# Quadratic attention inside a three-part kernel: the features are regrouped into four pairs of heads, and the second half's moments are taken earlier

## The reference, cut to what matters

```
q, k, v = split(x @ Wqkv.T + bqkv)            # 8 heads x 8 channels each
qn = normalize(q) * (scale * temperature); kn = normalize(k) * scale
v1 = [1, v]                                   # 9 columns a head
kv_mod[i,j,e] = sum_n kn_i kn_j v1_e / N      # moments of second degree
kv[d,e] = sum_n kn_d v1_e / N;  vsum[e] = sum_n v1_e / N
y = 0.5 * qn_i qn_j kv_mod[i,j,:] + scale^2 * qn_d kv[d,:] + scale^4 * vsum
out = (y[1:] / y[0]) @ Wproj.T + bproj
```

## Time and profile before

| | |
|---|---|
| median of 3 runs | 777.17 us (777.17 to 780.46) |
| profiled execution | 778.77 us |
| its span in the trace | 776.9 us |
| TensorE busy | 712.7 us, 92% |
| VectorE busy | 542.0 us, 70% |
| GpSimd busy | 439.9 us, 57% |
| ScalarE busy | 425.0 us, 55% |

### The profile page before, as it was taken

How to read it: one execution, slowest core, us unless ns; L and a number is a source line. 1 busy time by engine, 2 the same in 40 slices (tenths; PEclk the granted TensorE clock), 3 DMA queues, 4 the chain that set the end, 5 groups by cost and what they waited for, 6 DMA issues and landing times.

```text
span 776.9 us, 11085 instructions
## 1 busy us (share of the span) xinstructions
PE 712.7 (92%) x3474; PEld 354.0 (46%) x3474; DVE 542.0 (70%) x859; ACT 425.0 (55%) x763; POOL 439.9 (57%) x402
## 2 busy tenths in 40 slices
PE   5699999999999896869999999889999999999997
PEld 2345454544445453327777778523333333333332
DVE  2399899999899898775588888494444545454543
ACT  1788777878786885523455554544343333333342
POOL 1388777877787766845566666234443434343440
PEclk9799999999999997869999999999999999999999
DMA  4365465434444553331000000644944434443400
GB/s 132 128 165 148 128 155 143 123 95 114 111 123 124 132 131 82 80 87 24 2 1 4 3 5 3 128 94 93 183 99 108 99 75 92 107 105 77 89 1 21
DMA packets 30098, 70.20 MB, mean 90 GB/s; under 512 B 4483, under 2 KB 20175, under 8 KB 29647
## 3 DMA queue, kind: packets, MB, share of 16 engines
q1 hardware_dynamic: 29727, 68.77, 36.6%
q10 hardware_dynamic: 304, 0.63, 0.2%
HBM read 66.96 MB, written 2.43 MB: 89 GB/s over the span
## 4 chain that ended last, share of the span: by engine, by line
PE 46%; DVE 8%; issue 1%; ACT 1%; DVEq 0%; ACTq 0%
PE pair L849 22%; PE pair L930 11%; PE pair L790 5%; PE pair L773 3%; PE pair L826 2%; PE pair L813 1%; PE pair L835 1%; PE pair L841 1%; DVE big L1563 1%; DVE big L1567 1%; DVE big L1629 0%; DVE big L1628 0%; DVE big L1575 0%; DVE big L1568 0%; DVE big L1883 0%
## 5 line engine op out<-in xcount | busy, mean ns | idle before, releaser
L1726 DVE TENSOR_TENSOR hidden<-pair,tmp 128x502 f32<-128x502 f32 (+1 forms) x192 | 121.5, 674 | 127.4 <-PE pair L849 102.6
L1857 POOL TENSOR_TENSOR hidden<-xs,big 128x502 f32<-128x502 f32 (+1 forms) x96 | 111.9, 1167 | 163.4 <-PE pair L849 144.0
L1276 ACT ACTIVATE tmp<-pair 128x502 f32<-128x502 f32 (+1 forms) x192 | 102.4, 586 | 154.5 <-PE pair L849 154.5
L1883 POOL TENSOR_TENSOR big<-big 94x512 f32<-94x512 f32 (+3 forms) x120 | 89.2, 781 | 58.2 <-DVE big L1628 58.2
L849 PE MATMUL pair<-xs,w 64*128 64x502 f32 (+1 forms) x384 | 106.5, 631 | 0.0
L849 PE MATMUL pair<-hidden,w 64*128 64x502 f32 (+1 forms) x384 | 97.7, 585 | 4.3 <-DVE hidden L1726 3.3
L1418 DVE TENSOR_TENSOR_SCAN pair<-tmp,pair 128x750 f32<-128x750 f32 (+1 forms) x56 | 95.8, 1712 | 7.9 <-ACT tmp L1020 7.6
L930 PE MATMUL pair<-hidden,w 128*64 128x502 f32 (+1 forms) x384 | 91.1, 596 | 0.0
L1748 POOL TENSOR_TENSOR big<-big,work 128x750 f32<-128x750 f32 (+1 forms) x28 | 45.8, 1634 | 78.4 <-ACT big L994 78.4
L501 PE MATMUL pair<-big,work 128*128 128x512 f32 x112 | 62.2, 638 | 2.1 <-DVE work L1430 2.0
L849 PEld LDWEIGHTS pair<-hidden,w 64*128 64x128 f32 x384 | 36.6, 187 | 50.8 <-issue 46.1
(11 more groups left out here) (189 smaller groups left out, 1235.6 us busy)
## 6 DMA issues: line engine op xcount, KB each, us to landing
big<-dispatched SPq DMA_DIRECT2D x40, 502.0 KB, 6.6
spread<-rowsd SPq DMA_DIRECT2D x48, 375.0 KB, 5.6
spread<-rowsd SPq DMA_DIRECT2D x48, 187.5 KB, 3.3
big<-in_x SPq DMA_DIRECT2D x12, 375.0 KB, 6.3
big<-dispatched SPq DMA_DIRECT2D x8, 498.0 KB, 5.8
spread<-rowsd SPq DMA_DIRECT2D x8, 374.0 KB, 4.9
w<-in_w SPq DMA_DIRECT2D x5, 512.0 KB, 6.7
big<-in_x SPq DMA_DIRECT2D x1, 1500.0 KB, 8.1
```

What stands on the lines that cost most here:

```text
L1276: act.activation(sT[i % 4][:, 0:w], bank[BANK1[i]][:, 0:w], ACT.Silu).then_inc(silu_a, 1)
L1726: v.tensor_tensor(hidT[i % 8][:, 0:hi - lo], bank[BANK2[i]][:, 0:hi - lo], sT[i % 4][:, 0:hi - lo], ALU.mult)\
L1857: pool.tensor_tensor(xw[e % 4][:, 0:hi - lo], xs[:, lo:hi], wx[:, e, 0:hi - lo], ALU.mult)\
L1883: ins = eng.tensor_tensor(dst[:, :, at:at + H * m].rearrange("p u (h d) -> p u h d", d=m), t[:, :, :, 0:m], t[:, :, :, k:D], ALU.mult)
```

## The change

The features are regrouped by head: 36 products, 8 linear, 1 one for each head (HF = 45). A tile now holds two heads (FT = 90) and there are four tiles (FTN = 4). q, k and v lie in `qkv` with nine columns a head, the ninth a one, so that [v, 1] of two heads is 18 neighbouring columns.

- `moments(n)` swaps the operands: stationary are 32 columns of v and ones around a pair's 18, moving the 90 features of k; 16 products, four of them in a row each writing another 32 partitions of bank 4. Rows and columns that belong to other heads are multiplied by zero: VectorE multiplies once by `featw` (128x180) into `kvT`.
- `moments_turned(n)` is new on TensorE: two products `kvT`^T x `ksel` turn this back, pick each head's columns and copy the denominator to 8 columns. ScalarE copies the result into `kvm` (`moments(n)` on ScalarE, new).
- `q_features(n)`: 16 transposes and four copies.
- `attend(n)`: 16 products with a stationary 90x32 and 188 moving columns, four in a row each for another pair of heads and another 32 partitions of the bank. A stationary holds one sequence's 16 columns beside 16 of zeros; the two sequences are accumulated.
- `moments(2*att+1)` moves on TensorE and VectorE ahead of `project`, `gates`, `residual`, `logits` and `qk_sums`. It waits for ScalarE's copy of the first half's moments, since both halves now use bank 4.
- `wproj` has its rows by pair of heads and sequence and comes in 8 small transfers in place of 2; `featw` is built on GpSimd instead of loaded.

```diff
-QUAD = 288
-FEATS = QUAD + 72
-FT, FTN = 120, 3
+QUAD = 36
+HF = QUAD + D + 1
+FEATS = H * HF
+FT, FTN = 2 * HF, H // 2
+VW = 2 * (D + 1)
+VAT = [144 + VW * g - 14 for g in range(FTN)]
...
+            return (bank[2], bank[3], attended(n), bank[4 if n % 2 else 5])[f]      # features_bank(n, f)
...
             def moments(n):                                   # TensorE
...
-                if n % 2:
-                    after(pe, att_v, n - 1)
-                else:
-                    after(pe, kv_v, n - 1)
+                after(pe, kv_a, n)
+                after(pe, qt_a, FTN * n if n % 2 == 0 else 0)
                 for b in range(2):
-                    for f in range(FTN):
-                        for p in range(2):
-                            at = 65 * (FTN * b + f)
-                            mm = pe.matmul(bank[4 + n % 2][0:FT, at:at + 65],
-                                           kF[r % 2][0:rows, unit, FT * f:FT * f + FT],
-                                           qkv[r % 2][0:rows, unit, 143:208], start=(p == 0), stop=(p == 1))
+                    for p in range(2):
+                        for g in range(FTN):
+                            mm = pe.matmul(bank[4][32 * g:32 * g + 32, FT * b:FT * b + FT],
+                                           qkv[r % 2][0:rows, unit, VAT[g]:VAT[g] + 32],
+                                           kF[r % 2][0:rows, unit, FT * g:FT * g + FT], start=(p == 0), stop=(p == 1))
+            def moments_turned(n):
+                pe.wait_ge(fw_g, 3)
+                pe.wait_ge(kt_v, n + 1)
+                for b in range(2):
+                    mm = pe.matmul(bank[4][0:FT, 256 + 128 * b:384 + 128 * b], kvT[:, FT * b:FT * b + FT], ksel[:, :],
+                                   start=True, stop=True)
+                mm.then_inc(kc_p, 1)
...
             def attend(n):                                    # TensorE
                 for k in range(2):
-                    for f in range(FTN):
-                        for b in range(2):
-                            mm = pe.matmul(dst[64 * b:64 * b + 64, TOK * k:TOK * k + TOK],
-                                           kvm[n % 2][:, k, FTN * b + f, :], qT[n % 2][:, f, TOK * b:TOK * b + TOK],
-                                           start=(f == 0), stop=(f == FTN - 1))
+                    for b in range(2):
+                        for g in range(FTN):
+                            mm = pe.matmul(dst[32 * g:32 * g + 32, TOK * k:TOK * k + TOK],
+                                           kvm[n % 2][:, g, k, b:b + 2, :].rearrange("p b c -> p (b c)"),
+                                           qT[n % 2][:, g, TOK * b:TOK * b + TOK], start=(b == 0), stop=(b == 1))
...
             def attention():                                  # TensorE, order of a round
...
+                    if att is not None:
+                        moments_turned(2 * att)
+                        moments(2 * att + 1)
                     if ln2 is not None:
                         project(ln2)
                     if gate is not None:
                         gates(gate)
                     if att is not None:
-                        moments(2 * att + 1)
+                        moments_turned(2 * att + 1)
...
+            def moments(n):                                   # ScalarE
+                act.wait_ge(kc_p, n + 1)
+                after(act, at_p, n - 1)
+                src = bank[4][0:FT, 256:512].rearrange("p (b q c) -> p q b c", b=2, c=16)
+                dst = kvm[n % 2].rearrange("p g k b c -> p (g k) b c")[:, :, 0:3:2, :]
+                act.activation(dst, src, ACT.Copy).then_inc(kv_a, 1)
...
+                    if att is not None:                       # ScalarE, order of a round
+                        moments(2 * att)
                     if qkvs is not None:
                         qk_squares(qkvs)
                     if gate is not None and gate + 1 < NQ:
                         gate_exponentials(gate)
                     if qkvs is not None:
                         qk_norms(qkvs)
+                    if att is not None:
+                        moments(2 * att + 1)
                     if ln2 is not None:
                         second_squares(ln2)
...
             def moments(n):                                   # VectorE
                 v.wait_ge(kv_p, n + 1)
-                after(v, at_p, n - 1)
-                src = bank[4 + n % 2][0:FT, 0:2 * FTN * 65].rearrange("p (f c) -> p f c", c=65)
-                v.tensor_tensor(kvm[n % 2][:, 0], src[:, :, 1:65], featw[:, :, :], ALU.mult)
-                v.tensor_tensor(kvm[n % 2][:, 1], src[:, :, 0:1].to_broadcast([FT, 2 * FTN, 64]), featw[:, :, :],
-                                ALU.mult).then_inc(kv_v, 1)
+                after(v, kc_p, n)
+                v.wait_ge(fw_g, 2)
+                v.tensor_tensor(kvT, bank[4][:, 0:2 * FT], featw[:, :], ALU.mult).then_inc(kt_v, 1)
...
+                    if att is not None:                       # VectorE, order of a round
+                        moments(2 * att + 1)
                     if ln2 is not None:
                         residual(ln2)
                     if gate is not None:
                         logits(gate)
                     if qkvs is not None:
                         qk_sums(qkvs)
-                    if att is not None:
-                        moments(2 * att + 1)
```

More of the change, by code:

```diff
@@ L201, in features_bank, with of_heads @@
         def features_bank(n, f):
-            return attended(n) if f == FTN - 1 else bank[2 + f]
+            return (bank[2], bank[3], attended(n), bank[4 if n % 2 else 5])[f]
+        def of_heads(t, at, count):
+            return t[:, :, at:at + (D + 1) * count].rearrange("p u (h d) -> p u h d", d=D + 1)[:, :, :, 0:D]
         def dispatchT(r):
@@ L266, in program @@
             blk = slice(64 * k, 64 * k + 64)
-            later += [(wqkv[blk, 192 * k:192 * k + 192], a["wqkv"]), (wproj[blk, blk], a["wproj"]),
+            later += [(wqkv[blk, 192 * k:192 * k + 192], a["wqkv"]),
                       (gatew[blk, NE * k:NE * k + NE], a["gate_w"])]
@@ L271, in program @@
             (centering, "centering"), (averaging, "averaging"))]
-        later += [(featw[:, :, :], a["featw"]), (w3[:, :, :], a["w3"])]
-        PARAMS, LATER = 16 * len(first), 16 * len(later)
+        later += [(w3[:, :, :], a["w3"])]
+        blocked = [(wproj[32 * g + 16 * b:32 * g + 16 * b + 16, 64 * b:64 * b + 64], a["wproj"][16 * g:16 * g + 16, :])
+                   for g in range(FTN) for b in range(2)]
+        PARAMS, LATER = 16 * len(first), 16 * (len(later) + len(blocked))
         X_PARTS = [(750 * i, 750 * i + 750) for i in range(4)] + [(3000, 6000)]\
@@ L805, in q_features @@
                 for f in range(FTN):
-                    if f == FTN - 1:
+                    if f == 2:
                         after(pe, att_v, n - 1)
-                        if n % 2:
-                            pe.wait_ge(kv_v, n + 1)
+                    if f == 3 and n % 2:
+                        pe.wait_ge(kv_a, n + 1)
+                    elif f == 3:
+                        after(pe, att_v, n)
                     for b in range(2):
```

72 lines of the change are left out of this document (50 added, 22 removed).

## The result

The changed kernel takes 792.44 us (median of 4 runs, 791.41 to 793.67) against 778.28 us (4 runs) of the kernel before: a ratio of 1.0173, 95% interval 1.0146 to 1.0199, 13.5 us slower by the ratio and 14.2 by the medians. The forecast was 778.7 with a range of 769 to 787; the time lies above it. The rival of the lost clock is what happened, and was priced too low; some 3 us more came from outside the attention.

The account below looks back on a forecast made before the run. Full rounds were taken as bound by a chain over engines ending in VectorE's 8.9 us, not TensorE. Full rounds +1.3, t = 2 +0.8 and t = 9 -0.5 gave +1.6 us, so 778.7 us, range 769 to 787.

Parts of the forecast that it names:

- The rival of the lost clock: TensorE's new idle gaps drop its clock to 1.2 GHz in attention rounds: 782 to 787 us, chance 0.29.
- TensorE's work: Moments, turned products, q_features and attend together: -1.4 us for each half round, -22 us of TensorE's time over 16.
- the switches: Changes between whole and column-grouped products around the moments: 0.2 us going in, 0.1 coming out.
- The walk through a full round: Follows a full round's waits across engines: it grows from 19.36 to 19.7 us, +1.3 over four.
- front chain: First half of a round, projection, bias, squares, sums, norms up to k's scaling; forecast to end 0.1 us later.
- TensorE's 22 us: TensorE's saved time over 16 half rounds, the gain if TensorE set the end everywhere.
- its bound: Round t = 2: +0.8 us, up to +2.5 if the clock stays low.
- the 2.15 us ahead of the one fall: TensorE's busy time from 353.01 to 356.42 in the earlier trace, before 3.42 us at 1.2 GHz.
- transposes count for less: Skill's claim that transposes don't count as busy for the clock the same way; the new round has more of them.
- TensorE still sets the rounds: Rival: shorter waits let the -22 us through, wholly 757 us, half 767; chance 0.19.
- The four column groups don't run together: Rival: groups run two at a time in moments and attend, about 3 us a round, 801 us; chance 0.04.
- the hand-over of the bound: Main forecast: full rounds stay set by VectorE's chain and new waits, no lost clock, 775 to 782 us; chance 0.43.

Follow-up runs that it names:

- e3_move: Kernel before with only the second half's moments moved ahead of project and gates (TensorE) and residual, logits, sums (VectorE): 800.8 us, ratio 1.0275.
- e4_bank: Changed kernel with the second half's moments in bank 5 instead of bank 4, so they don't wait for ScalarE's first copy: 785.41 us, ratio 1.0097.
- e6_order: e4_bank with VectorE's qk_sums ahead of residual and logits, ScalarE's squares ahead of the first moments' copy, gate exponentials later: 780.48 us, ratio 1.0024.
- e1_fill: Changed kernel with idle 128x128 by 128-column products, results unread, put into TensorE's waits throughout the attention: 783.04 us, ratio 1.0077.
- e8_one_fill: Changed kernel with idle products only in a round's longest wait, ahead of second_variance (4, or 2 at t = 3): 788.23 us, ratio 1.0105.
- e7_order_fill: e6_order plus fewer idle products than e1_fill, none ahead of the second moments: 775.02 us, ratio 0.9960.
- e2_back: Changed kernel with the second half's moments put back behind project and gates on TensorE and qk_sums on VectorE: 797.85 us, ratio 1.0255.

## Why the prediction was wrong, point by point

- *TensorE's work.* Right. Moments were put at 0.64 us and the switches; the timeline has 0.76 from L810 to the next L795. `attend` saves 0.65 (put at 0.64), the turned products take 0.44. Busy time fell by 2.8 us a full round, as summed (1.4 for each half). The moments that run by column groups take 0.83 us for 32 records with their tail. The Trainium skill ("TensorEngine Tiling (Array Packing)", "Instruction Overhead"), weighed there, has about 60 cycles a product, which was put at 25 ns a record: in L810 four records start within 0.02 us and the next fours mostly 0.08 us apart, some 20 ns a record, so the trace doesn't agree where four column groups run together.
- *The walk through a full round.* Right in kind and within 0.3 us in size: 19.41 for the 19.7 put. The wait for ScalarE's copy was put at 0.73, is 0.56; VectorE's for the second moments at 1.3, is 1.30; `project` at 5.6 us, is 5.51; the sums at 8.0, are 7.91. e3_move and e4_bank change the front chain alone, and the full rounds follow: 2.3 us more, 0.6 less, each close to what was put down for it. e6_order makes the best round 1.2 us shorter still and the last full one not at all. That TensorE's 22 us come through nowhere held: with the clock held, the attention is 0.2 us shorter, for +1.6 forecast. The sum was off by 1.0 us in the four full rounds (+0.3 for +1.3) and by 0.9 in t = 2 (-0.1 for +0.8), so the forecast would have been too high here, not too low.
- *The clock* is the step that failed. The sum that gave 778.7 holds no lost clock at all: it was a term of nothing, for the reasons that the new gaps are 1.6 and 0.7 us long with a product between them and that all rounds from t = 3 on had kept 1.00. Those reasons don't hold: the changed kernel has waits of 1.05 to 1.37 and 0.79 us with a product between them, and loses the clock in t = 4, 7, 8 and 9. As a rival the prediction gave it 0.29, "0.5 to 1 us in a round, in 7 rounds 3.5 to 7" and 782 to 787 in all. e1_fill shows 9.7 us in the attention. As a rival the mechanism was named right, with its place in the full rounds (TensorE's new wait ahead of `second_variance`, e8_one_fill). Its frequency in the full rounds was even lower than put, two of four; its price was not. I let a fall last as long as the one of the earlier trace rows and took the slack off it. Of the four falls one was so short (461.0 to 464.4) and cost 0.9 us; the one of 6.8 us cost 2.3; t = 2 lost 2.05 and t = 8 and 9 together 4.35 (10.2 and 17.1 us at half clock). I had given t = 8 and 9 no price of their own beside the 0.5 to 1 us of any round, and t = 2 its bound only in passing. And its chance was put at 0.29, although the new stretch, put at 1.8 us busy of 3.4, holds less work than the 2.15 us ahead of the one fall that the prediction goes by the earlier trace rows. The first stage of the same trace has more, and it cuts both ways: 1.53 us busy of 3.42 ahead of a fall, and 1.73 of 3.41 with none behind it:

```profile
318.88:322.29 3.41, 1.73 (x7) 0.65 (x4) 3.01 (x5) 2.83 (x5) 2.02 (x2) 1.00 0.56 134
322.29:325.70 3.41, 3.38 (x11) 1.82 (x11) 3.38 (x3) 0.81 (x2) 3.25 (x3) 1.00 0.51 125
325.70:329.12 3.42, 1.53 (x6) 0.75 (x6) 2.95 (x4) 2.32 (x4) 3.36 (x6) 0.99 0.42 100
329.12:332.53 3.41, 3.41 (x6) 1.41 (x5) 3.31 (x5) 0.38 (x1) 1.63 (x1) 0.51 0.00 0
```

  The changed kernel has, ahead of its fall at 399.5 and after it:

```profile
396.12:399.53 3.41, 1.61 (x11) 0.81 (x9) 2.48 (x6) 2.63 (x9) 0.82 (x1) 1.00 0.00 0
399.53:402.94 3.41, 3.05 (x33) 1.96 (x34) 3.27 (x6) 1.90 (x5) 3.41 (x5) 0.50 0.00 0
```

  That transposes count for less, which the prediction weighed too, is tested by no run.
- *What lies outside the attention.* The forecast plus the clock's 9.7 us, less the 1.8 us by which the rest of the attention's sum was too high, is 786.6, still inside the range; the last miss comes from outside. +2.0 us before the first round were not forecast (0 to +1) and are not explained. Over the profiles of this study the first round begins at 343.4, 343.6 and 346.6 us with the setup of before, and between 342.4 and 349.9 with the changed one (11 profiles, middle 345.4). So one execution's start says little; whether 1 us or more belongs to the change is open, and so are the last 1.1 us behind the attention and the 4.5 us by which e1_fill's median stays above the kernel before.
- *The rivals.* "TensorE still sets the rounds" is refuted by e3_move and e4_bank. "The four column groups don't run together" is refuted by L810 and L858.

So the hand-over of the bound was described rightly, and the case that came on top of it, the clock, was put down as the less likely one. Taking 15% of TensorE's work out of a full round, from between waits that stay, changed here its clock and not the length of a round at full clock.

## What to carry to other kernels

Before less work on TensorE is called harmless, list its waits in the new schedule, all rounds, the first and the last ones too, and price the clock there by what half speed does to the chain that is bound elsewhere. If a round is set by a chain over several engines, find the one order in it that everything waits for (here the sums of squares), and put it first; taking work off the busiest engine moved nothing, and giving each half its own bank and the sums an earlier place moved 1.8 us in the best full round and 1.3 on average. Idle products in waits were worth 9 us here by the medians; in e7_order_fill full rounds that kept the clock anyway were 0.5 us longer with them. Try them first in rounds that lose the clock.

## What the runs showed of the hardware that I had not expected

- A stretch at 1.2 GHz can last much longer than the first row suggests: 17.1 us (481.4 to 498.5) in rounds in which TensorE was at work for 85% and 86% of the time. The four falls of the changed attention last 10.2, 6.8, 3.4 and 17.1 us; what ends one is not shown.
- Products whose results nobody reads bring an attention whose full rounds TensorE doesn't set from 162.7 to 153.0 us, in one profiled execution each.
- In e3_move TensorE is idle for 2.6 us of a full round (busy 19.07 of 21.68) and keeps the clock from t = 3 to 7; in e2_back, with one wait of 2.17 us and 17.18 busy of 20.46, it loses it in every full round.
- Three rounds of the changed kernel with the same waits and the same 1.57 us of work in the same 3.41 us part: two keep the clock, one loses it.
